# A graph network with mixed dense and gathered aggregation: ten destination tiles held as dense adjacency in place of eleven

## The reference, cut to what matters

```python
cnt = zeros((3125, 4)).at[dst, edge_type].add(1.0)
inv_deg = 1.0 / maximum(cnt[dst, edge_type], 1.0)          # 100000 edges, 4 relations
for l in range(4):                                          # rgcn layer, X is 3125 x 256
    h = einsum('ni,rio->rno', X, W[l])
    msg = h[edge_type, src] * inv_deg[:, None]
    out = segment_sum(msg, dst, 3125) + X @ root[l] + bias[l]
    X = elu(layernorm(out) * gamma[l] + beta[l]) + X
x = x + X
# then a mixture of 8 experts, top 2 of 8 per node: 256 -> 512 (gelu) -> 256, weighted by a softmax
```

## Time and profile before

| | |
|---|---|
| median of three executions | 2982.96 us (2974.68 to 3000.87) |
| the profiled execution | 2987.39 us, its span 2985.6 us |
| TensorE busy | 2263.2 us (76%), 16512 matmuls |
| VectorE busy | 1692.1 us (57%) |
| GpSimd busy | 1552.0 us (52%) |
| ScalarE busy | 822.0 us (28%) |
| dense steps, four layers | 4400 matmuls, 1164.7 us busy |
| chunks, four layers | 4800 matmuls, 381.2 us busy |
| gathers | 1200, 1213.1 us busy, 1011 ns each |

### The profile page before, as it was taken

One profiled execution on the slowest core, in us unless ns is written; L12 is line 12 of the kernel. 1 busy time (PEld: TensorE's weight loads), 2 busy tenths in 40 slices (PEclk: granted clock), 3 DMA queues, 4 the chain that ended last, 5 costly groups with the idle time before them and its releaser, 6 DMA issues.

```text
span 2985.6 us, 49222 instructions
## 1 busy us (share of the span) xinstructions
PE 2263.2 (76%) x16512; PEld 1358.5 (46%) x16512; DVE 1692.1 (57%) x5722; ACT 822.0 (28%) x1695; POOL 1552.0 (52%) x1660
## 2 busy tenths in 40 slices
PE   0677788878897788888978887887867776846992
PEld 0234444445443344445534444554444444425881
DVE  6947666656664455565535465553657656663334
ACT  2744343534562011111111111110111111114771
POOL 2777665665320566666236666644667665122221
PEclk9888888979898889999988999999889887867996
DMA  4687343434323666665456566655665544212224
GB/s 125 175 248 235 76 121 114 125 112 118 88 105 99 185 203 192 186 191 181 148 162 216 189 207 198 200 175 157 205 202 163 149 128 143 82 45 66 73 73 150
DMA packets 215200, 448.67 MB, mean 150 GB/s; under 512 B 42478, under 2 KB 138722, under 8 KB 213287
## 3 DMA queue, kind: packets, MB, share of 16 engines
q1 hardware_dynamic: 136023, 261.82, 28.4%
q0 software_dynamic: 67168, 172.52, 19.5%
q10 hardware_dynamic: 11760, 11.08, 1.4%
HBM read 344.26 MB, written 100.70 MB: 149 GB/s over the span
## 4 chain that ended last, share of the span: by engine, by line
PE 47%; DVE 14%; issue 14%; DMA 12%; another core or an unknown queue 5%; ACT 3%; POOL 3%; SPq 1%; ACTq 0%; DVEq 0%; POOLq 0%
PE n_PS L1743 23%; PE n_PS L1784 8%; PE n_PS L1764 6%; DMA n_yg<-n_BIG,n_IDX 6%; PE n_PS L1714 5%; PE n_PS L1780 2%; DMA n_BIG<-n_xd,n_SIDX 2%; DVE n_ST L1530 2%; DMA n_xg<-n_tabs,n_INVA 2%; DVE n_OW L1441 2%; POOL n_BIG L1345 1%; DVE n_BIG L1427 1%; PE n_PS L1688 1%; PE n_PS L1759 1%
## 5 line engine op out<-in xcount | busy, mean ns | idle before, releaser
L1345 POOL DMA_INDIRECT n_BIG<-n_xd,n_SIDX x1200 | 1213.1, 1011 | 833.3 <-issue 281.8
L1743 PE MATMUL n_PS<-n_BIG 125*128 125x500 f16 x4400 | 1164.7, 400 | 96.8 <-issue 59.4
L1743 PEld LDWEIGHTS n_PS<-n_BIG 125*128 125x128 f16 x4400 | 410.4, 103 | 505.2 <-issue 197.9
L1764 PE MATMUL n_PS<-n_OW,n_BIG 128*128 128x116 f16 (+24 forms) x4800 | 381.2, 211 | 133.3 <-issue 99.9
L1764 PEld LDWEIGHTS n_PS<-n_OW,n_BIG 128*128 128x128 f16 x4800 | 311.8, 102 | 329.3 <-issue 168.8
L1784 PE MATMUL n_PS<-n_BIG,n_tabs 128*128 128x256 f16 x2400 | 319.8, 289 | 37.6 <-issue 36.0
L1441 DVE TENSOR_SCALAR n_OW<-n_io,n_tabs 128x116 f16<-128x116 f16 (+24 forms) x1200 | 219.1, 271 | 182.6 <-PE n_PS L1764 123.9
L1530 DVE TENSOR_TENSOR n_ST<-n_PS,n_INVB 128x500 f32<-128x500 f32 x200 | 199.3, 1037 | 165.8 <-issue 93.4
L1784 PEld LDWEIGHTS n_PS<-n_BIG,n_tabs 128*128 128x128 f16 x2400 | 247.6, 104 | 95.2 <-issue 54.4
L1714 PE MATMUL n_PS<-n_BIG,n_tabs 128*128 128x500 bf16 x576 | 175.1, 413 | 79.6 <-ACT n_BIG L1216 30.4
L1427 DVE TENSOR_SCALAR n_BIG<-n_io,n_tabs 128x500 bf16<-128x500 f16 x576 | 185.9, 374 | 77.7 <-PE n_PS L1714 43.5
(11 more groups left out here) (258 smaller groups left out, 2548.3 us busy)
## 6 DMA issues: line engine op xcount, KB each, us to landing
n_BIG<-n_a SPq DMA_DIRECT2D x160, 625.0 KB
n_a<-n_BIG SPq DMA_DIRECT2D x11, 3125.0 KB
n_xg<-n_tabs SPq DMA_DIRECT2D x53, 481.9 KB
n_INVB<-n_ind SPq DMA_DIRECT2D x100, 250.0 KB
n_BIG<-n_xd,n_SIDX POOLq DMA_INDIRECT x1200
n_BIG<-in_L_ffn_W_dram SPq DMA_DIRECT2D x32, 512.0 KB
n_xd<-n_BIG SPq DMA_DIRECT2D x75, 112.0 KB
n_whl<-n_BIG SPq DMA_DIRECT2D x16, 512.0 KB
```

Source lines behind the costliest of these rows:

```text
L1345: e.indirect_dma_start(m.GR[:, g % GS, :], None, m.XD[l % 2][:, :], bass.IndirectOffsetOnAxis(ap=m.SIDX[:, i:i + 1], axis=0)).then_inc(s[f ...
L1743: ins = e.matmul(m.bank(2 * p + h, 0, W), m.xps[l % 2][0:TN, part, D * k + 128 * h:D * k + 128 * h + 128], m.RA[0:TN, c.slot_of(n), W * (k ...
L1764: ins = e.matmul(m.bank(2 * p + h, at, c.width[q]), m.GR[:, g % GS, D * part + 128 * h:D * part + 128 * h + 128], ow, start=False, stop=Fa ...
```

## The change

`NEAR` goes from 11 to 10, so tile 10 (nodes 1250 to 1374) becomes a far tile. One f16 matrix of ones, `ON16`, is dropped and `ALL1` (now f16 in place of bf16, as are `PRE` and `SEL`) serves in its place, which frees SBUF; two scratch areas move. The order list follows from the planner, which is not changed itself.

```diff
-NEAR = 11
+NEAR = 10
...
-        self.ON16 = sb("ON16", [128, 128], F16)
...
-        self.CMP = raf[:, 8800:9300]
-        self.GAB = raf[:, 9300:9300 + 2 * L * D].rearrange("p (w l d) -> p w l d", w=2, l=L)
+        self.CMP = raf[:, 8800:9400]
+        self.GAB = raf[:, 9400:9400 + 2 * L * D].rearrange("p (w l d) -> p w l d", w=2, l=L)
...
-        self.PRE = sb("PRE", [128, 128], BF16)
-        self.ALL1 = sb("ALL1", [128, 128], BF16)
-        self.SEL = sb("SEL", [128, 2, E8], BF16)
+        self.PRE = sb("PRE", [128, 128], F16)
+        self.ALL1 = sb("ALL1", [128, 128], F16)
+        self.SEL = sb("SEL", [128, 2, E8], F16)
...
-    k.did(e.memset(m.ON16[:, :], 1.0))
...
-        counts, one = (m.DK[:, t % 2, r:W:R], m.ON16[0:T, 0:1]) if t < c.TD else (m.CNT[:, r:W:R], m.onef[0:1, :])
+        counts, one = (m.DK[:, t % 2, r:W:R], m.ALL1[0:T, 0:1]) if t < c.TD else (m.CNT[:, r:W:R], m.onef[0:1, :])
...
-    ins = e.matmul(m.bank(7, at, c.width[q]), m.ON16[:, :], ow, start=False, stop=False, skip_group_check=True)
+    ins = e.matmul(m.bank(7, at, c.width[q]), m.ALL1[:, :], ow, start=False, stop=False, skip_group_check=True)
```

More of the change, by code:

```diff
@@ L826, in prep_scalar @@
         e.activation(m.halves(0, t)[0], m.X[0:TN, t, :], ACT.Copy, scale=m.scale[0:TN, 0:1]).then_inc(s["hi0"], 1)
-N_CONST = 22
+N_CONST = 21
 def prep_gpsimd(e, c, m, s):
```

## The result

Ten dense tiles take **1.0153** times the time of eleven (95% interval 1.0115 to 1.019): 3025.18 us median (3020.89 to 3031.72, four runs) against 2978.82 (2968.63 to 3000.87, four runs). The forecast was 2950, faster by 1.1%. The profiled execution of the changed kernel has a span of 3019.2 us, 33.6 more than before.

A forecast was written before the change was run, and what follows sets the result against it. It took TensorE's order to set the pace of the chunk stretches, not GpSimd's gathers. Layer 0's -24 and routing's -9 make -33 us: 2987.4 profiled gives 2954, with the median 4.4 lower a forecast of 2950 us, range 2911 to 3000.

The forecast's parts named there:

- The pivot: Layers 1 to 3: gathers could run at 1.32 us, 14% faster, so TensorE's order sets 1.53 us a chunk.
- the gathers set the pace: Rival, chance 0.18: GpSimd's gathers set layers 1 to 3, dense steps only fill; 327 chunks cost +57 us, so 3007.
- Layer 0: Dense steps and pairs without gathers, TensorE-bound at the end: less TensorE work, -24 us, bounds -18 to -30.
- Layer 0 to 1: Last product's end to first chunk: 35.0 us in place of 20.8, the store standing behind the weights' maximum and loads.
- Layer 1: First to last chunk: 433 us for 289 chunks, then 39 us for 38 standing alone; product's end 5 us earlier.
- Layer 2: First to last chunk: 452 us for 290 chunks, then 38 us for 37 standing alone; product's end unchanged (0).
- the factor of 1.42: Layer 1's measured 459.5 us over 324 us of TensorE work, applied to the changed kernel's 306 us to give 433.
- The lone chunks: Ends of layers 1 and 2: 38 and 37 chunks without dense steps, bound by gathers at 1.32 us, about 39 us each.
- The sign that I had named for a wrong mechanism: Layer 1, before the chunks that stand alone: a pace well off 1.50 us a chunk would show a wrong mechanism.
- Layer 3: First to last chunk: 321 us of TensorE work times 1.67, so 537 us where it was 503.1.
- Routing: After layer 3's last chunk: 43 us (30 to 60 possible) to the 18th tile's logits; end at 2694 against 2704, -9 us.
- The clock: TensorE's clock, 0.52 in routing, halves after idleness; chunks standing alone could make the sum up to 6 us longer.

The follow-up runs named there:

- the store-first kernel: Ten dense tiles with the last tile's `low` ahead of `wmax` and its store ahead of `wput` at the ends of layers 0 and 1: 1.0011 on the 2670 us chip.

## Why the prediction was wrong, by its steps

- **The pivot failed.** "GpSimd idled ... 57.8 us on TensorE's chunks, which is the ring of 12 slots being full. Without that last part a gather takes ... 1.32 us. So GpSimd could go 14% faster than it does, and the order of TensorE is what sets 1.53." With half the dense matmuls it did not go faster at all. The name of the releaser was in most cases the last semaphore that had moved, not a wait. The test was in the trace: a ring that is full holds a gather until just after the chunk twelve before it, and that one had ended 4.5 us earlier (median of the late ones). From this step the forecast priced the stretches by TensorE's work, 472, 490 and 537 us, where 488.9, 499.9 and 562.3 were measured. The rival "the gathers set the pace" (chance 0.18) had 501, 508 and 548 us, 1557 in all; measured are 1551. Its 3007 missed the layers' ends.
- **Layer 0**, -24: measured -25.5. The only stretch where TensorE was full, and the sum of its work came out; no run takes it apart.
- **Layer 0 to 1**, 35 us from product to chunk: 39.6; the first gather was 36 us behind the product, not 28. The mechanism (store behind the maximum and the loads) was right; the 34 dense steps that I counted as useful there were no gain, if dense work inside the stretches costs nothing, as the runs with half of it say.
- **Layer 1**, 433 + 39: 440.7 + 48.2. **Layer 2**, 452 + 38: 452.8 + 47.1. The first parts are near by luck: the factor of 1.42 only restated the measured 1.5 us a chunk, and the dense steps beside a chunk hardly changed. The lone chunks show the error: priced at 1.32 us a gather, they take 1.5 (30 gathers in 44 us). In all +27 against the forecast, and 2 to 3 us more from the last chunk to the product. The sign that I had named for a wrong mechanism, a pace off 1.50 us before the lone chunks, could not tell the theories apart (it was 1.52): both gave 1.5. The lone chunks could.
- **Layer 3**, 537: 562.3, the largest miss (+25). 327 chunks at the old 1.68 are 548; the other 14 us stay unassigned, between routing and the gathers behind it.
- **Routing**, 43 us from the last chunk to the 18th tile's logits: 49.9, inside my 30 to 60. Eight tiles behind the last product, as said.
- **The sum**: -33 forecast, +33.6 measured in the profiles. Of the 67 between them, 52 lie in the three stretches.
- **The clock** (0.52 in routing, up to 6 us): 0.72 in the lone chunks. That these are held by the gathers fits their length; no run prices the clock in them.

## What to carry to other kernels

Before pricing work on the busiest engine, cut that work in half and look whether the stretch moves: a producer that is busy for 76% (323 of 425 us, on the 2670 us chip) can still be the one that paces everything. A wait that names an engine proves nothing until the time between that engine's event and the waiting instruction is near zero. Work beside a stretch that it does not set costs little to put in, while there is room, and is worth little to take out; the gain lies in moving work into it (2991.8 to 2926.4 us, -2.2% here) and in starting the stretch earlier. For the start, look at everything that stands in order ahead of its first step: a gather that goes out sooner gains little where a product ahead of the first chunk is late.

## What the runs showed of the hardware

- A gather's starts lie 1.25 us apart where nothing disturbs it (0.95 and 0.30 of idle), on every chip. On the slower chips, long intervals come between:

```profile
1204.67 0.94 POOL L1345 DMA_INDIRECT n_BIG<-n_xd,n_SIDX  x1 [0.30 <-issue]
1205.92 0.96 POOL L1345 DMA_INDIRECT n_BIG<-n_xd,n_SIDX  x1 [0.30 <-issue]
1207.19 0.94 POOL L1345 DMA_INDIRECT n_BIG<-n_xd,n_SIDX  x1 [0.30 <-issue]
1208.43 0.94 POOL L1345 DMA_INDIRECT n_BIG<-n_xd,n_SIDX  x1 [0.30 <-issue]
1211.14 0.94 POOL L1345 DMA_INDIRECT n_BIG<-n_xd,n_SIDX  x1 [1.76 <-PE n_PS L1764]
```

These rows are of the kernel before. In its layer 1, 56 of 299 intervals are over 1.9 us and make 71.7 us more than 1.25 each would; on the 2670 us chip, in the store-first kernel, 11 of 326 and 11.0 us. TensorE shows such pauses too, as "issue": in layer 1 of the kernel before 35.6 us in 72 gaps before matmuls that wait for no semaphore, and none over 0.1 us in the store-first kernel on the 2670 us chip. With ten tiles the long intervals make 66.7 us in layer 1 on the slower chip, 55.7 more than on the faster, and the stretch is 65.1 us longer there. So they are most of the difference between the chips in that layer; what makes them stays open.
- A store of 125 KB that is issued behind weights and dense tiles on SyncE's queue lands 14 us later, ahead of them within 3 us. The gathered rows, which are on GpSimd's queue, had then landed 6.1 us after the first gather, beside the weights and tiles; the median in layer 1 of the kernel before is 3.2 us.
